# A transformer block's tail rewritten: residual on TensorE, last pass on ScalarE, one norm for two batches

## The reference

```python
x = layernorm(x + attention(x))      # 16 heads of 64, rotary position, softmax, output projection
x = layernorm(x + experts(x))
# experts(x), for each token:
gates = softmax(x @ gate_w)          # 8 experts
topk_g, topk_i = top_k(gates, 2)
tok_w = topk_g.sum()                 # one weight for both chosen experts
h = gelu(x @ w1[e] + b1[e])          # 64 wide, for all 8 experts
y = h @ w2[e] + b2[e]
out = tok_w * sum over the two chosen e of y[e]
# layernorm(v) = (v - mean) / sqrt(var + eps), with no gain and no offset
```

## Time and profile before

| what | value |
|---|---|
| median of 3 executions | 236.6 us (233.94 to 241.07) |
| the profiled execution | 236.22 us |
| its span, first to last instruction | 234.4 us |
| mean granted TensorE clock | 0.953 |
| busy over the span: PE, DVE, ACT, POOL | 75%, 80%, 68%, 65% |
| attention up to 190 us: DVE busy | 157.9 of 190 us |
| tail from 190 to 222 us: PE busy | 28.8 of 32 us |
| end from 222 us: DVE busy | 8.4 of 12.4 us |

### The profile page before, as it was taken

How to read it: one execution, slowest core, us unless ns; L and a number is a source line. 1 busy time by engine, 2 the same in 40 slices (tenths; PEclk the granted TensorE clock), 3 DMA queues, 4 the chain that set the end, 5 groups by cost and what they waited for, 6 DMA issues and landing times.

```text
span 234.4 us, 5256 instructions
## 1 busy us (share of the span) xinstructions
PE 174.9 (75%) x1823; PEld 124.3 (53%) x1823; DVE 186.6 (80%) x541; ACT 160.1 (68%) x330; POOL 151.5 (65%) x127
## 2 busy tenths in 40 slices
PE   1788774497768869875876887578878879986970
PEld 0223353274646656654665666456656656765660
DVE  6989873869698897969889896988897757749393
ACT  3869687198579779957986996785669884354300
POOL 6060979997797988778798978998300400224951
PEclk9999999589999988999999999999999988999795
DMA  7133503121216212121221312122100000000112
GB/s 247 56 90 90 137 15 82 34 57 37 57 38 175 72 47 70 36 57 35 60 59 46 77 42 57 34 59 64 29 1 2 4 3 0 3 0 0 45 49 90
DMA packets 13002, 12.63 MB, mean 54 GB/s; under 512 B 3152, under 2 KB 11952, under 8 KB 12976
## 3 DMA queue, kind: packets, MB, share of 16 engines
q1 hardware_dynamic: 12512, 11.77, 18.9%
q10 hardware_dynamic: 464, 0.52, 0.7%
HBM read 2.73 MB, written 1.05 MB: 16 GB/s over the span
## 4 chain that ended last, share of the span: by engine, by line
DVE 30%; POOL 26%; PE 22%; ACT 7%; DMA 7%; issue 5%; ACTq 1%; POOLq 0%; DVEq 0%
POOL by_cos L1014 12%; POOL by_sin L1014 12%; DVE row_max L1188 9%; DVE roped L1149 7%; DMA qk<-mT_sb 5%; PE ps_o L592 4%; PE ps_s L554 4%; DVE o_sb L1211 3%; ACT raw L816 3%; PE ps_m L496 3%; PE ps_t L448 2%; DVE oT_sb L1241 2%; DMA in_b<-in_packed_b 2%; ACT probs L851 1%; DVE hs L1408 1%
## 5 line engine op out<-in xcount | busy, mean ns | idle before, releaser
L851 ACT ACTIVATE probs<-ps_t 128x512 bf16<-128x512 f32 x128 | 77.0, 617 | 34.6 <-PE ps_t L448 34.0
L1188 DVE TENSOR_REDUCE row_max<-ps_s 128x2 bf16<-128x512 f32 x120 | 80.3, 674 | 13.8 <-PE ps_s L396 11.9
L1014 POOL TENSOR_TENSOR by_cos<-raw,in_b 128x1024 bf16<-128x1024 bf16 x26 | 55.1, 2120 | 18.1 <-DVE roped L1149 16.8
L396 PE MATMUL ps_s<-qk 128*128 128x256 bf16 x218 | 43.0, 281 | 20.4 <-DVE row_max L1188 19.7
L816 ACT ACTIVATE raw<-ps_m,bqk 128x256 bf16<-128x256 f32 x128 | 53.3, 487 | 4.8 <-PE ps_m L381 4.8
L448 PE MATMUL ps_t<-qk 128*128 128x256 bf16 x256 | 50.4, 281 | 7.4 <-DMA qk<-mT_sb 7.0
L1014 POOL TENSOR_TENSOR by_sin<-raw,in_b 128x1024 bf16<-128x1024 bf16 x26 | 55.2, 2122 | 0.0
L469 PE MATMUL ps_o<-v_sb,probs 128*128 128x65 bf16 x512 | 36.6, 196 | 1.3 <-DVE o_sb L1211 0.9
L469 PEld LDWEIGHTS ps_o<-v_sb,probs 128*128 128x128 bf16 x512 | 31.9, 99 | 7.5 <-ACT probs L851 1.2
L381 PE MATMUL ps_m<-in_b 128*128 128x256 bf16 x128 | 27.7, 308 | 8.8 <-DMA in_b<-in_packed_b 4.3
L448 PEld LDWEIGHTS ps_t<-qk 128*128 128x128 bf16 x256 | 23.4, 100 | 13.7 <-DMA qk<-mT_sb 9.2
(11 more groups left out here) (129 smaller groups left out, 248.4 us busy)
## 6 DMA issues: line engine op xcount, KB each, us to landing
qk<-roped SPq DMA_DIRECT2D x124, 64.0 KB, 2.0
in_b<-in_packed_b SPq DMA_DIRECT2D x1, 768.0 KB, 5.8
out<-y_sb SPq DMA_DIRECT2D x3, 256.0 KB, 2.2
in_f<-in_packed_f SPq DMA_DIRECT2D x1, 586.0 KB, 4.1
in_b<-in_packed_b SPq DMA_DIRECT2D x1, 512.0 KB, 4.4
in_b<-in_packed_b ACTq DMA_DIRECT2D x1, 256.0 KB, 3.7
qk<-mT_sb SPq DMA_DIRECT2D x16, 4.0 KB, 1.7
bv_rep<-in_repeated_bv SPq DMA_DIRECT2D x1, 256.0 KB, 2.8
```

Source lines behind the costliest of these rows:

```text
L396: mm = nc.tensor.matmul(ps_s[h % 2][:, t * S:t * S + S], qk[:, u % 4, 0, h % 4, h // 4, t * P:t * P + P], qk[:, u % 4, 1, h % 4, h // 4, : ...
L851: nc.scalar.activation(probs[:, h % 4].rearrange("p c s -> p (c s)"), ps_t[h % 2][:], ACT.Exp, scale=DH ** -0.5).then_inc(exp_done, 1)
L1014: last = nc.gpsimd.tensor_tensor(by[:, g].rearrange("p a h s -> p (a h) s"), raw[:, u % 2, g].rearrange("p a h s -> p (a h) s"), table[:]. ...
L1188: nc.vector.tensor_reduce(row_max[:, u % 2, h % 4, h // 4, :], of_head[:].rearrange("p (t s) -> p t s", s=S), AX_X, ALU.max, negate=True). ...
```

## The change

Nothing changes up to slot 13. From there on:

- **Residual on TensorE.** `experts_out` adds x1 by one more product of the transposed `x1T` with the identity, in the same accumulation. `residual` and `z` go; `moments` reads the PSUM bank.
- **Last pass on ScalarE.** `moments` also makes the negated mean, GpSimd multiplies it by the inverse deviation to `shift`, and ScalarE's new `normed(p)` makes `y * rs + shift` from PSUM for pieces 0 to 4. Piece 5 stays VectorE's. `y_sb` holds all 16 tiles, so nothing waits for a store; a bank is now free when ScalarE has done its last pass.
- **One norm for batches 6 and 7.** `out_proj(7)` writes beside `out_proj(6)` in `ps_m[0]`, and `ln_one` and `inverse_deviation` run once over four tiles.
- **Other banks.** The transposes of batch 7 go to `ps_o`, both copies are ScalarE's (`read_oT(7, 1)` was VectorE's), and `spread_weights` uses only `ps_t`.
- **New order.** The routing of batches 4 and 5 (`logits(1)`, `route(1, ...)`, `gate_exp(1)`) moves ahead into slots 14 and 15; `turn_weights(0)` and `hidden(1)` move out of slot 15. The lists behind the slots are written anew on PE, DVE, ACT and POOL.

The core of the diff:

```diff
             def experts_out(tc, t):
                 if t == 0:
-                    need(pe, z_step, Z_STEPS * (tc - 2) + 1)
+                    need(pe, y_out, tc - 1)
...
                 if p >= 4:
-                    take(5 - p, z_step, Z_STEPS * p + 1)
+                    take(5 - p, y_out, p + 1)
...
                 nc.tensor.matmul(y, wtT[:, tok:tok + P], b2_p[:], start=True, stop=False)
+                nc.tensor.matmul(y, x1T[:, tok:tok + P], id_sb[:], start=False, stop=False)
...
+            def normed(p):
+                first, count = PIECES[p]
+                act.wait_ge(shift_ready, p + 1)
+                for t in range(count):
+                    last = nc.scalar.activation(y_sb[:, first + t, :], PIECE_BANKS[p][:, t * HID:t * HID + HID],
+                                                ACT.Identity, scale=rs2[:, first + t:first + t + 1],
+                                                bias=shift[:, first + t:first + t + 1])
+                last.then_inc(y_out, 1)
...
                 if k == 3:
                     read_oT(LAST, 0)
-                if k == 8:
+                if k == 4:
+                    read_oT(LAST, 1)
+                if k == 9:
+                    read_weights(1)
+                if k == 11:
                     read_x1T(2)
-                if k == 11:
+                    normed(0)
                     gate_exp(2)
-                    read_weights(1)
-                if k == 13:
+                if k == 14:
                     read_weights(2)
+            for p in range(1, LAST_PIECE):
+                normed(p)
...
-            for r in (1, 2):
-                for k in range(10, G_STEPS + 1):
-                    route(r, k)
             for p, (first, count) in enumerate(PIECES):
...
+                pool.wait_ge(y_step, Y_STEPS * (p + 1))
+                nc.gpsimd.tensor_tensor(rs2[:, tiles], ve2[:, tiles], mhalf[:, 0:count], ALU.pow).then_inc(rs2_ready, 1)
+                if p < LAST_PIECE:
                     pool.wait_ge(rs2_ready, p + 1)
...
+                    nc.gpsimd.tensor_tensor(shift[:, tiles], minus_mean[:, tiles], rs2[:, tiles],
+                                            ALU.mult).then_inc(shift_ready, 1)
+                if p == 0:
+                    for k in range(10, G_STEPS + 1):
+                        route(2, k)
...
-                nc.vector.tensor_tensor(z[:, p % 2, 0:count], y, x1[:, first:first + count, :], ALU.add).then_inc(z_step, 1)
...
                 for t in range(count):
+                    last = nc.vector.bn_stats(st2[:, first + t, :], PIECE_BANKS[p][:, t * HID:t * HID + HID])
+                last.then_inc(y_step, 1)
...
+                if p < LAST_PIECE:
+                    nc.vector.tensor_scalar(minus_mean[:, tiles], mv2[:, tiles, 0], -1.0, None, ALU.mult)
```

More of the change, by code:

```diff
@@ L697, in slot @@
                     hidden(3)
-                if T == 15:
-                    turn_weights(0)
-                    hidden(1)
                 if s["attend"]:
@@ new lines, in moments, with normed @@
+                last.then_inc(y_step, 1)
+                dve.wait_ge(y_step, Y_STEPS * p + 2)
+                if p < LAST_PIECE:
+                    nc.vector.tensor_scalar(minus_mean[:, tiles], mv2[:, tiles, 0], -1.0, None, ALU.mult)
+                nc.vector.tensor_scalar(ve2[:, tiles], mv2[:, tiles, 1], EPS, None, ALU.add).then_inc(y_step, 1)
+            def normed(p):
+                first, count = PIECES[p]
+                dve.wait_ge(rs2_ready, p + 1)
+                for t in range(count):
+                    last = nc.vector.tensor_scalar(y_sb[:, first + t, :], PIECE_BANKS[p][:, t * HID:t * HID + HID],
+                                                   mv2[:, first + t, 0:1], rs2[:, first + t:first + t + 1],
+                                                   ALU.subtract, ALU.mult)
+                last.then_inc(last_out, 1)
@@ L1451, in _ @@
+            for k in range(6):
+                weigh(k)
+            ln_one(LAST - 1, 1)
             weigh(6)
-            ln_one(LAST, 4)
+            ln_one(LAST - 1, 2)
+            ln_one(LAST - 1, 3)
             weigh(7)
-            for k in range(3, 10):
-                route(1, k)
-            route(2, 1)
-            route(2, 2)
-            residual(0)
+            ln_one(LAST - 1, 4)
             moments(0)
@@ L1461, in _ @@
             weigh(9)
+            route(2, 1)
+            route(2, 2)
+            weigh(10)
+            weigh(11)
             for k in range(3, 10):
                 route(2, k)
-            weigh(10)
-            weigh(11)
-            residual(1)
             moments(1)
```

226 lines of the change are left out of this document (99 added, 127 removed).

## The result

| | kernel before | changed kernel |
|---|---|---|
| median | 236.76 us (233.94 to 241.07) | 228.06 us (227.46 to 229.75) |
| ratio, with its 95% interval | 1 | 0.9682 (0.9576 to 0.9788) |
| profiled execution, and its span | 236.22, 234.4 us | 227.77, 226.0 us |
| mean granted clock | 0.953 | 0.973 |

The forecast was 226.5 us, in a range of 222.5 to 231.5. The change saves 8.7 us by the medians and 8.4 us by the spans of the two profiled executions. The four executions of the changed kernel read 227.77, 227.46, 228.34 and 229.75.

A forecast was written before the change was run, and what follows sets the result against it. TensorE, with its waits and low clock, was taken to bound the tail. Span 234.4 - 1.3 - 6.1 - 2.75 + 0.5 = 224.75 us; against the profiled execution of 236.22 the forecast is 226.5, range 222.5 to 231.5.

The forecast's parts named there:

- Start of the tail, -1.3: First spread_weights starts at 189.15 instead of 190.44 us, as batch 6's norm leaves VectorE between transposes and weights copy.
- The walk on ScalarE and GpSimd up to the last routing: Step-by-step times from the joint norm through piece 0's last pass (0.39 a tile) and table load; routing ends at 211.6.
- TensorE through the tail, -6.1: First spread to last expert product: 29.1 us of work plus 1.5 of waits, 30.6 instead of 36.6.
- other waits 0.15: TensorE's remaining waits in the tail, beside 0.25 before the last routing's transposes and 1.1 before the last group.
- most ahead of the last group: Expected profile sign: TensorE idle under 2 us from the first spread on, most of it before the last group.
- After the last product, -2.75: Last product to VectorE's last pass takes 2.5 us instead of 5.25, GpSimd's queue of powers and shifts setting the end.
- End behind the last pass: After VectorE's last pass, the store's landing takes 2.1 us, the same as in the kernel before.
- Low clock, +0.5: Low clock after TensorE's idle time before the new tail, taken as 0.5 us between 0 and 1.8.
- the rival on the clock: TensorE stays at its lower clock level for half the tail's work, giving 240 us; chance 0.04.
- The wait moved into the routing: Piece 0 comes late, so TensorE waits 3 us for the last routing, giving 229.5 us; chance 0.22.
- The bank held: Last group waits for its PSUM bank until piece 1's late last pass, giving 233.5 us; chance 0.08.
- The last piece no shorter: GpSimd's queue replaces VectorE's; at upper-bound costs the end takes 3.5 instead of 2.5, 227.5, inside the forecast's 0.66 case.

The follow-up runs named there:

- e5: Changed kernel with separate norms for batches 6 and 7; tail stretch (last mT_sb copy to end of span) 47.98 us as in the changed kernel, median 227.01 us.
- e7: Changed kernel with residual and last passes both back on VectorE, new order, banks and joint norm kept; tail stretch 50.42 us, median 228.80 us.
- e1: Changed kernel with only the residual back on VectorE; tail stretch 49.26 us against 47.98, median 229.20 us.
- e2: Changed kernel with all last passes back on VectorE, reading PSUM, residual still on TensorE; tail stretch 50.17 us against 47.98, median 230.99 us.
- e9: e8 with the last piece's store issued by ScalarE's DMA queue; tail stretch 47.53 us, median 228.05 us.
- after_again: Changed kernel run and profiled once more, unchanged; tail stretch 47.96 us, median 226.94 us.
- e8: Changed kernel with three steps of routing moved off VectorE's queue ahead of the copy of the first weights; tail stretch 47.79 us, median 227.34 us.
- e10: Changed kernel with four extra unused ScalarE activations ahead of piece 0's last pass; tail stretch 49.17 us, medians 226.66 and 230.11 us.
- e4: Kernel before with fourteen unread products filling two TensorE idle gaps; tail stretch 54.82 us against 57.61, median 233.73 us.
- e3: Changed kernel with eight extra unused ScalarE activations ahead of piece 0's last pass; tail stretch 52.00 us, median 231.99 us.
- before_again: Kernel before run and profiled once more, unchanged; tail stretch 56.49 us against 57.61 first, 237.50 us (one execution).
- e6: Kernel before with residual on TensorE and last pass on ScalarE, old order kept; tail stretch 60.51 us against 57.61, median 240.71 us.

## Why the prediction was right

Going by its own steps; times of its walk are counted 1.23 us later, since the attention ended so much later in the profile after.

*Start of the tail, -1.3: right in size,* -1.30, *and right by half in its reason.* The copy starts at 189.54 (walk 188.4 + 1.23 = 189.63). The transposes still wait for GpSimd's routing, 0.78. The prediction gave all of the gain to the norm that leaves VectorE. TensorE's and VectorE's timelines of before say otherwise:

```profile
187.93 0.81 PE L554 MATMUL ps_s<-x1T,w_p 128*128 128x512 bf16 x3
188.58 0.53 PE L469 MATMUL ps_o<-v_sb,probs 128*128 128x65 bf16 x12
```

```profile
188.90 0.18 DVE L1202 RECIPROCAL r_sum<-ps_o 128x4 f32<-128x4 f32 x1 [1.98 <-PE ps_o L469]
189.00 0.70 DVE L1234 TENSOR_SCALAR x<-ps_m,mv,rs 128x128 bf16<-128x128 f32 x2
```

The norm's last step holds VectorE from 189.00 to the copy at 189.62, 0.62 us. Ahead of it VectorE waited for a product that stood behind `hidden(1)`, 0.65 us, and `hidden(1)` now comes behind that product. The two are 1.27 of the 1.30; no run parts them. e5 shows that joining the norms has no part in it.

*The walk on ScalarE and GpSimd up to the last routing: right.* Piece 0's power starts at 203.78 (203.63 by the walk), the table load at 206.76 (206.58), and GpSimd's routing ends at 212.92 (212.83). The last pass, which no trace showed, was put at 0.39 a tile between 0.265 and 0.487; it is 0.38. The load starts 0.02 behind the last pass and takes 1.28, so the rows were the better guide here than the 2.66 us for a switch on the Trainium skill's page "ScalarE: Activation LUTs", section "What ACT_TABLE_LOAD costs".

*TensorE through the tail, -6.1: 0.67 too much.* The work of 29.1 stands; the term that was too small is the waits, 1.5 us, which are 31.17 - 29.1 = 2.07. Of these, `wt_p` of the last group is nil instead of 0.25 (213.23, no wait; 0.25 in e7). The last group has some 0.9 instead of 1.1: 0.27 at 216.10, 0.41 at 216.82, and 0.09 in each of two tiles ahead. The failed step is "other waits 0.15": from start to start these small gaps, as at 191.83, come to about 1.2 us. Most lie ahead of `turn_weights(2)`, which starts 22.86 us behind the first spread with 21.8 of work before it; they make TensorE late enough that `wt_p`, ready at 212.92, is no longer waited for. (The walk's own time for this point, 211.35, is 0.4 above 189.15 + 21.8, without a term for it.) The walk let each engine start as soon as its input was ready; whether these gaps are the queue behind a spread or GELU that is just being done, as I take them to be, no run shows. The sign "most ahead of the last group" did not come.

*After the last product, -2.75: -3.44, right in time, by two errors that cancel, and wrong as a difference.* I said that GpSimd's queue sets the end, at 221.7, and that VectorE's pass ends at 222.1. It ended at 222.90 and 223.35, that is 221.67 and 222.12 in the walk's time. But GpSimd began at 219.37, 0.64 later than the 217.5 of the walk, and took 3.53 us instead of 4.2 (the walk's own durations add to 3.9), so the agreement is luck. This chain hangs on the last `weigh`, over moments, four powers and three `shift`, and not on the last product. So TensorE's extra 0.7 us cost nothing: the last product moved into the end's shadow, and used it up, as VectorE has piece 5's `ve` at 222.27 and GpSimd is free for it at 222.35. By e1 the move of the residual pays at the end (1.17 of 1.28 us); by e2 that of the last pass pays in both places, 1.29 there and 1.47 on TensorE.

*End behind the last pass, "as before": mis-sized by 0.54.* 2.65 us instead of 2.11. ScalarE's pass of piece 4 now ends at 223.25 and VectorE's of piece 5 at 223.35, and both stores go through SP's queue one behind the other. e9 gets 0.26 of it back by a second queue, and e2, whose last two passes end 0.76 apart, has 2.09. I had put the end of piece 4's pass at 221.5, which is 222.73 here. Its `shift` is done at 222.35, so that isn't what it waits for: ScalarE does pieces 2 to 4 in one row from 220.70 on, when it has the first `shift`, and comes to piece 4 at 222.77.

*Low clock, +0.5: nil here.* The granted clock is 1.00 from 190 to 222 us in the profile of the changed kernel, and in those of after_again, e1, e2, e5, e7, e8, e9 and e10 as well. e4 and e3 show that waits and low clock belong together: filling the first gap takes low clock away, a wait of 2.20 brings it. One reading in the rival on the clock was wrong: the 1.09 us of four fp32 products at 214.23 isn't work at the lower level. Before_again has the same 1.09 at 216.55 with the clock at 1.00.

*The forecast's own base: +1.23.* This is what separates 224.75 from 226.0, together with +0.67, -0.69, +0.54 and -0.5 from above. The forecast took before's profiled execution as a base, and its attention part was 1.3 us shorter than the mean of fourteen. With that mean, the same terms give 227.8, beside medians of 228.06 and 226.94. Why the granted clock fell to 0.83 between 60 and 70 us in one execution and not in the other stays open.

*The rivals.* The wait moved into the routing: not in this kernel, but its slack is only 0.4 us, and e3 shows 4.0 us for 2.75 of delay. The bank held: not in this order, but 0.89 in e2 and 6.83 and 0.80 in e6, so this was the real danger of the change. Lower level: no. The last piece no shorter: GpSimd's queue did take VectorE's place, and at 1.81 against 5.25 us it is still the shorter one.

So the time went, in the tail: 7.2 us by the new order with its banks and buffers, 2.4 by moving residual and last pass, nothing by the joint norm. Of the 7.2 us up to 2.8 are low clock (e4), which differs from one execution to the next: against before_again it is 6.1 and 1.7, and 4.4 us are left either way. These are differences of whole kernels; the order's share was not split further, between TensorE's list, the early copy of the weights, VectorE's list, the buffers that no longer wait for a store, and GpSimd's passes.

## What to carry to other kernels

A move to another engine is priced with the order around it: the same two moves are worth -2.44 us in one order and +2.90 in the other, where a last pass that reads PSUM holds the bank that TensorE needs. When one engine bounds a stretch, walk its list against the others' with start-to-start times, and add a small gap (here 1.2 us over 31) for every place where it meets another engine closely. Before a difference of 1 us is explained, cut the span at one instruction that all variants share, and take each kernel's trace twice: behind that cut the changed kernel repeats to 0.02 us and the kernel before, with its low clock, only to 1.12, while what is ahead scatters by 3.5.

## What the runs showed of the hardware that I had not expected

- The tail stretch of three executions (47.98, 47.96, 47.98) agrees to 0.02 us, from the same code in two cases and from another norm in the third.
- A wait on TensorE does not always bring low clock: 1.70 us was followed by 0.66 and 1.62 us by 1.00 in two executions of the same kernel; 2.20 us was followed by 0.74 and 0.80 us by 1.00 in e3 and e10.
- Idle work paid: fourteen unread products made the kernel before faster, by 2.8 us of its tail stretch, or 1.7 against its second execution.
- A store's issue takes 0.36 us of the queue it is issued on (median of six).
- Two stores of 64 KB that are ready 0.1 us apart end 0.5 us later than one, 2.65 against 2.11 us, though each lands in about 1.8 us.
